# One table of slot numbers placed anew in a single-core layer kernel: jobs and statistics of the first stretches and the last stages

## The chip, the cores and the metric

The kernel runs on one core of one Trainium2 chip. The metric is the device time of one execution in microseconds (us). Three runs of the kernel before took 1712.45, 1713.23 and 1714.37 us; their median is 1713.23 us. The profiled execution is the one of 1712.45 us.

The core has a matrix engine (PE, with its weight loads shown as PEld), a vector engine (DVE), a scalar engine (ACT), a third elementwise engine (POOL) and a queue that issues DMAs (SP). Each engine takes its own instructions in the order in which they are written, and waits on semaphores for the others.

## The reference

Input is x of 4 batches x 2048 positions x 256 features, in float32. What is computed:

```
x = x + 0.5 * ffn(layernorm(x))
x = x + attn(layernorm(x))
x = x + 0.5 * ffn(layernorm(x))

ffn(z)  = z @ W.T + b + (z @ V_r) @ C.T            # 256 -> 256, rank 32
attn(z): q, k, v = split(z @ W_attn)               # 16 heads of 16
  s = (q @ k.T) / 4, causal
  p = (s*s + 1)/1000 for s > 0;  (1 - s/100)/1000 for -100 <= s <= 0
  return (p @ v) @ W_proj
```

There is no division by a row sum, so the attention of a tile can be added up in any order.

## The kernel before, in words

**Chunks and stages.** The 8192 positions are cut into 16 chunks of 512 (four to a batch). Each chunk goes through three stages. Stage A loads x, computes the first layer norm and feed-forward part, then the second layer norm. Stage B projects to q, k and v, splits q and k into three bf16 parts (`split`), and computes per 128 positions a "state", the sum of k times v, from which the linear part of the score function is later formed. Stage C takes the attention's output, projects it, adds x, and computes the third layer norm and second feed-forward part.

**Attention.** It is cut into 64 visits (a batch, a group of 4 heads, a chunk of queries), and a visit into tiles of 128 keys by up to 512 queries; there are 640 tiles, and each is done in two **halves** of 2 heads. For a half, PE writes scores into one of two score buffers (`score<-qs,ks`), then DVE or ACT raises them into `rp` (L1222 on DVE, L1093 on ACT); the next half but one can't be scored until that is done. Tiles on the diagonal need a second operation per head (`lin`, L1228 or L1099) and masks on POOL (L960). Then the raised tile is squared on ACT (L1109, L1113) and, for shared tiles, half of it on POOL (L985), and three tiles later PE multiplies it by v (`y_ps<-rp,vt`). In this text H with a number is a half: tile T consists of H = 2T and 2T + 1.

**Jobs.** Everything else that PE does is a job: z1T, z2T, z3T (transposes of a normalised chunk, L1317), ffn, qT, k, v, kT, state, proj, out. A job is written in pieces into one of two PSUM banks (`bank`), and emptied from it by ACT or DVE. A job can't start before the job two places ahead of it has been emptied. Emptying a `state` (L1208 on DVE) waits for the addition of the state two before it on POOL (L1011, L1013). The statistics of a layer norm are a row of small steps, one slot each, from the slot named `ln1`, `ln2` or `ln3` on: four on DVE (L1247), at +4 the aggregation (L1164), at +6 a square root on ACT (L1122), at +8 a reciprocal on DVE (L1168; for ln2 also the shift, L1171), at +9 to +12 four steps on POOL: for ln2 the normalisation `z` (L945), for ln1 and ln3 the adding of the bias to x (L955).

**The order of the work.** It is written out by hand in slots. `order()` lays a line of slots; in each slot an engine first empties the banks that are due, then does its part of the half in that slot, then its other work, and on PE half, values, then pieces of jobs. A slot has no time: it only says what stands behind what on an engine, and an empty slot costs nothing. The tables give, for each stage, at which slot after the stage's start a job or a layer norm starts. `A_FIRST`, `A_SECOND`, `B_FIRST`, `A_EARLY` and `B_EARLY` serve the first chunks, `A_FULL`, `B_FULL` and `C_FULL` the steady part, which repeats every 80 slots (one half in each), and `C_HALF`, `C_LATE` and `C_SHORT` the last stages, whose starts are in `LATE`. `HALVES_AFTER` says over which slots the first 32 halves are spread; after them every slot holds a half:

```
    first = at + HALVES_AFTER[0]
    second = at + HALVES_AFTER[1]
    halves = 2 * QUADS * NB
    o.put_halves([first + (second - first) * i // halves for i in range(halves)])
```

All later stages are laid relative to `second`.

Of the kernel before, what the change touches and what calls it, by code (L numbers as in the profile page):

```python
# [169 lines left out]

A_FULL = {"z1T": (30, 31), "ffn": (37, 39), "z2T": (64, 64), "ln1": 21, "ln2": 48}
B_FULL = {"qT": (0, 5), "k": (7, 10), "v": (15, 19), "kT": (35, 43), "state": (51, 61, 63, 66)}
C_FULL = {"proj": (22, 26), "ln3": 58, "z3T": (67, 67), "out": (71, 75)}
A_FIRST = {"z1T": (2, 3), "ffn": (6, 10), "z2T": (26, 27), "ln1": 0, "ln2": 15}
A_SECOND = {"z1T": (15, 16), "ffn": (28, 32), "z2T": (49, 50), "ln1": 10, "ln2": 37}
A_EARLY = {"z1T": (12, 13), "ffn": (16, 20), "z2T": (38, 39), "ln1": 5, "ln2": 24}
B_FIRST = {"qT": (0, 12), "k": (2, 6), "kT": (10, 14), "v": (17, 20), "state": (24, 25, 26, 27)}
B_EARLY = {"qT": (4, 6), "k": (7, 8), "kT": (14, 15), "v": (26, 28), "state": (34, 35, 36, 37)}  # L180
C_HALF = {"proj": (0, 7), "ln3": 11, "z3T": (12, 12), "out": (22, 26)}
C_LATE = {"proj": (0, 4), "ln3": 13, "z3T": (9, 10), "out": (18, 24)}
C_SHORT = {"proj": (0, 4), "ln3": 9, "z3T": (9, 10), "out": (18, 22)}


LENGTHS = (36, 51, 42)
HALVES_AFTER = (36, 33)


PLACES = (9, 47, 14, 80)  # L190
ENDS = 3
LATE = (1053, 1086, 1146, 1196, 1231)

AGGR, SCALES, ROOT, NORM, BIAS = NB, NB + 4, NB + 2, NB + 5, NB + 5

# [77 lines left out]
def order():  # L273
    o = Order()
    o.stage(0, o.stretch(LENGTHS[0]), A_FIRST)
    at = o.stretch(LENGTHS[1])
    o.stage(0, at, B_FIRST)
    o.stage(1, at, A_SECOND)
    first = at + HALVES_AFTER[0]
    third, fourth, steady, period = PLACES  # L280
    at = o.n
    o.stage(1, at, B_EARLY)
    o.stage(2, at, A_EARLY)

    second = at + HALVES_AFTER[1]
    halves = 2 * QUADS * NB
# [3 lines left out]
    for c, at in ((2, third), (3, fourth)):  # L290
        o.stage(c, second + at, B_EARLY)
        o.stage(c + 1, second + at, A_EARLY)
    for c in range(CPB, NCH):
        step = c - CPB + 1
        o.stage(c, second + steady + period * step, B_FULL)
        if c + 1 < NCH:
            o.stage(c + 1, second + steady + period * step, A_FULL)
        if step >= ENDS:
            o.stage(step - ENDS, second + steady + period * step, C_FULL)
    done = NCH - CPB + 1 - ENDS  # L300
    for c in range(done, NCH - 1):
        o.stage(c, second + LATE[c - done], C_HALF if c < NCH - 2 else C_LATE)
    assert o.next_half == 2 * len(WORK)
    o.drain = o.n
    o.stretch(LAG + 9)
    o.stage(NCH - 1, o.stretch(32), C_SHORT)
    o.again = o.n
    for c in range(NCH, 2 * NCH):
        o.stage(c, o.stretch(40), C_SHORT)
    o.finish()  # L310
# [1182 lines left out]
```

## Time and profile before

| what | value |
|---|---|
| median of three runs | 1713.23 us |
| profiled execution, its own time | 1712.45 us |
| its span in the trace | 1710.7 us |
| PE busy | 1592.4 us (93%) |
| ACT busy | 1368.1 us (80%) |
| DVE busy | 1327.1 us (78%) |
| POOL busy | 1247.7 us (73%) |
| chain that ended last, by engine | PE 69%, DVE 17%, ACT 7%, issue 4%, POOL 3% |
| mean granted PE clock | 0.988 of full |

The span is the time from the first to the last instruction in the trace; 1.75 us of the execution lie outside it. A share of the span is an average over stretches with different limits, so it has to be read stretch by stretch. A gap of PE in the timeline names what released it. The granted clock (PEclk) is 1.00 at 2.4 GHz and 0.50 at 1.2 GHz.

### The profile page before, as it was taken

The page shows a single profiled execution, that of the slowest core. Times are in us where ns is not written, and L with a number is a line of the kernel's source. Part 1 is how long each engine was busy: PE and PEld are TensorE (multiplying, and loading weights), DVE is VectorE, ACT ScalarE, POOL GpSimd, SP SyncE. Part 2 cuts the span into 40 slices and gives each one's busy share as a digit, 9 for nine tenths or more (in the row PEclk, how much of TensorE's full clock was granted, in tenths as well). Part 3 has the DMA queues.
Part 4 walks back from the last instruction along what each step waited for, and adds up shares of the span by engine and source line. Part 5 has one row for each costly group of instructions (what it writes and reads, how often), then busy time and mean ns, then how long its engine had stood idle before and what let it go on. Part 6 is the DMA issues. An engine that isn't in the chain of part 4 may idle for free.

```text
span 1710.7 us, 67555 instructions
## 1 busy us (share of the span) xinstructions
PE 1592.4 (93%) x27158; PEld 813.7 (48%) x27158; DVE 1327.1 (78%) x3276; ACT 1368.1 (80%) x2182; POOL 1247.7 (73%) x1319
## 2 busy tenths in 40 slices
PE   5698999999998999999998999999999899999997
PEld 3353444444455545545455554544445554444443
DVE  4577777878788787887878678787878768788885
ACT  2366778899887888888887888898888789788883
POOL 1577687877778787776868787687777878667663
PEclk8899999999999999999999999999999999999999
DMA  2654643423346453333435544334333545323311
GB/s 88 180 165 117 179 133 96 128 86 120 89 114 180 140 154 113 114 107 94 131 107 168 162 118 132 116 100 131 124 109 106 162 137 155 105 81 85 91 46 55
DMA packets 183381, 206.16 MB, mean 121 GB/s; under 512 B 27164, under 2 KB 157076, under 8 KB 181276
## 3 DMA queue, kind: packets, MB, share of 16 engines
q1 hardware_dynamic: 183068, 201.77, 39.9%
q8 instruction: 222, 3.64, 0.9%
q14 instruction: 91, 0.75, 0.1%
HBM read 123.26 MB, written 76.30 MB: 117 GB/s over the span
## 4 chain that ended last, share of the span: by engine, by line
PE 69%; DVE 17%; ACT 7%; issue 4%; POOL 3%; DMA 0%; SPq 0%; ACTq 0%; POOLq 0%; DVEq 0%
PE y_ps L1289 26%; PE score L1289 21%; PE bank L1289 18%; DVE rp L1222 11%; PE bank L1317 3%; DVE lin L1228 3%; ACT rp L1093 2%; ACT rp L1113 2%; DVE bnst_ln L1247 1%; POOL rp L985 1%; ACT rp L1109 1%; PE bank L1359 1%; DVE x L1186 1%; ACT parts L1073 0%; POOL z L945 0%
## 5 line engine op out<-in xcount | busy, mean ns | idle before, releaser
L1222 DVE TENSOR_SCALAR rp<-score 128x512 f32<-128x512 f32 (+3 forms) x1728 | 965.0, 585 | 266.2 <-PE score L1289 262.2
L985 POOL TENSOR_TENSOR rp<-rp 128x1024 f32<-128x1024 f32 (+3 forms) x416 | 723.5, 1747 | 97.6 <-DVE rp L1222 86.2
L1289 PE MATMUL score<-qs,ks 96*32 96x512 bf16 (+3 forms) x10240 | 722.6, 349 | 53.4 <-DVE lin L1228 29.9
L1289 PE MATMUL y_ps<-rp,vt 128*16 128x512 f32 (+3 forms) x5120 | 594.4, 532 | 13.5 <-ACT rp L1113 5.1
L1093 ACT ACTIVATE rp<-score 128x512 f32<-128x512 f32 (+3 forms) x832 | 439.8, 570 | 203.6 <-PE score L1289 200.2
L1289 PEld LDWEIGHTS score<-qs,ks 96*32 96x32 bf16 x10240 | 295.4, 96 | 430.8 <-DVE rp L1222 191.6
L1109 ACT ACTIVATE rp<-rp,rise 128x1024 f32<-128x1024 f32 (+3 forms) x416 | 444.2, 1096 | 4.7 <-POOL rp L960 4.7
L960 POOL TENSOR_SCALAR_AFFINE_SELECT rp<-rp 128x256 f32<-128x256 f32 (+1 forms) x384 | 184.6, 481 | 239.8 <-ACT rp L1093 149.1
L1113 ACT ACTIVATE rp<-rp 128x2048 f32<-128x2048 f32 (+2 forms) x224 | 328.9, 1468 | 3.4 <-POOL rp L960 3.3
L1228 DVE SCALAR_TENSOR_TENSOR lin<-score,slope_mask 128x128 f32<-128x128 f32 x768 | 214.0, 279 | 0.0
L1289 PEld LDWEIGHTS y_ps<-rp,vt 128*16 128x16 f32 x5120 | 137.6, 96 | 105.3 <-issue 19.9
L1289 PE MATMUL bank<-w_qkv,z2T 128*32 128x256 f32 x2048 | 151.5, 379 | 0.8 <-ACT parts L1073 0.8
L1289 PE MATMUL y_ps<-lin,vt 128*16 128x128 f32 x2048 | 106.3, 274 | 0.0
L1289 PEld LDWEIGHTS y_ps<-lin,vt 128*16 128x16 f32 x2048 | 62.4, 96 | 80.0 <-issue 67.5
L1289 PEld LDWEIGHTS bank<-w_qkv,z2T 128*32 128x32 f32 x2048 | 68.0, 109 | 68.0 <-issue 43.8
L568 POOL TENSOR_TENSOR parts<-rest,parts 128x512 bf16<-128x512 f32 x56 | 65.5, 1170 | 44.2 <-ACT parts L570 43.2
L1289 PE MATMUL bank<-w_out,y_c 128*32 128x256 f32 x1024 | 77.9, 379 | 1.6 <-DMA y_c<-y_sb 1.6
L1289 PE MATMUL bank<-w_ffn,zT 128*32 128x256 f32 x1024 | 74.6, 393 | 3.6 <-DVE st_add L1208 2.1
L1289 PE MATMUL bank<-w_ffn,z3T 128*32 128x256 f32 x1024 | 76.9, 379 | 0.8 <-ACT z3T L1048 0.8
L566 POOL TENSOR_TENSOR rest<-qkT,parts 128x512 f32<-128x512 f32 x56 | 65.7, 1173 | 15.5 <-ACT parts L1073 15.3
L1099 ACT ACTIVATE lin<-score 128x128 f32<-128x128 f32 x256 | 75.5, 295 | 0.0
L1289 PE MATMUL y_ps<-qT,st 66*16 66x128 f32 x2048 | 68.9, 272 | 1.8 <-issue 1.8
(93 smaller groups left out, 1258.1 us busy)
## 6 DMA issues: line engine op xcount, KB each, us to landing
ks<-part_scratch SPq DMA_DIRECT2D x648, 64.0 KB, 2.4
qs<-part_scratch SPq DMA_DIRECT2D x384, 64.0 KB, 2.4
part_scratch<-parts SPq DMA_DIRECT2D x14, 1536.0 KB, 6.0
vt<-v_scratch SPq DMA_DIRECT2D x102, 128.0 KB, 2.7
state_scratch<-st_new SPq DMA_DIRECT2D x16, 528.0 KB
x_sb<-in_L_attn_x_dram SPq DMA_DIRECT2D x16, 512.0 KB, 4.3
x_scratch<-x SPq DMA_DIRECT2D x16, 512.0 KB, 5.3
qT_scratch<-qkT SPq DMA_DIRECT2D x16, 512.0 KB, 3.3
```

The lines of the kernel that those rows point to most:

```text
L566: ins = eng.tensor_tensor(rest[side][:], qkT[:, i, :], parts[:, i, 0, :], ALU.subtract)
L568: ins = eng.tensor_tensor(parts[:, i, 2, :], rest[side][:], parts[:, i, 1, :], ALU.subtract)
L960: pool.affine_select(out=block, in_=block, compare_op=ALU.is_ge, fill=fill, base=0, pattern=[[0, heads_in_it], [1, P]], channel_multiplier ...
L985: pool.tensor_tensor(half, half, half, ALU.mult).then_inc(squared["pool"], 1)
L1093: nc.scalar.activation(rp[T % RP_BUFS][:, 2 + v, off:CH], score[H % S_BUFS][:, v, off:CH], ACT.Relu).then_inc(raised["act"], 1)
L1099: nc.scalar.activation(lin[D % L_BUFS][:, 2 + v, :], score[H % S_BUFS][:, v, off:off + P], ACT.Copy, scale=SLOPE, bias=ONE).then_inc(lin_d ...
L1109: nc.scalar.activation(part, part, ACT.Square, bias=rise[:]).then_inc(squared["act"], 1)
L1113: nc.scalar.activation(whole, whole, ACT.Square).then_inc(squared["act"], 1)
L1222: nc.vector.tensor_scalar(rp[T % RP_BUFS][:, 2 * u + v, off:CH], score[H % S_BUFS][:, v, off:CH], 0.0, RISE, ALU.max, ALU.add).then_inc(ra ...
L1228: nc.vector.scalar_tensor_tensor(lin[D % L_BUFS][:, 2 * u + v, :], score[H % S_BUFS][:, v, off:off + P], ONE / SLOPE, slope_mask[:, 0, :], ...
L1289: return nc.tensor.matmul(*args, start=start, stop=stop, skip_group_check=True)
L1317: ins = nc.tensor.transpose(dst[:, P * blk:P * blk + P], src[:, blk, P * i:P * i + P], ident[:])
```

## The change

Numbers in the tables are changed, and nothing else: no instruction is added or taken out on any engine, and no line of code but these is touched.

```
-A_FULL = {"z1T": (30, 31), "ffn": (37, 39), "z2T": (64, 64), "ln1": 21, "ln2": 48}
+A_FULL = {"z1T": (31, 31), "ffn": (37, 39), "z2T": (64, 64), "ln1": 21, "ln2": 48}
-C_FULL = {"proj": (22, 26), "ln3": 58, "z3T": (67, 67), "out": (71, 75)}
+C_FULL = {"proj": (22, 26), "ln3": 60, "z3T": (67, 67), "out": (71, 75)}
...
-HALVES_AFTER = (36, 33)
+HALVES_AFTER = (37, 41)
...
-LATE = (1053, 1086, 1146, 1196, 1231)
+LATE = (1053, 1084, 1148, 1197, 1231)
```

`HALVES_AFTER` spreads the first 32 halves over 55 slots (73 to 127) where it was 48 (72 to 119), while the jobs of chunks 1 and 2 in that stretch keep their slots. So fewer halves stand ahead of each of these jobs: z2T of chunk 1 starts behind H7 where it was H9, its qT behind H11 (H13), its first state behind H28 (H33), and z2T of chunk 2 behind H31, both parts in one slot (H37 and H38). In A_FIRST, ln2 moves by 1 slot and z2T by 2, with no other work between; in A_SECOND, ln1 moves from 10 to 14.

In the early stages from then on, A_EARLY has z1T at (13, 14) for (12, 13) and z2T at (39, 39) for (38, 39), and B_EARLY v at (24, 28) for (26, 28) and the states at (34, 35, 37, 37) for (34, 35, 36, 37). In the last stages, C_HALF has out at (24, 28) for (22, 26), C_LATE z3T at (10, 10) for (9, 10) and out at (20, 26) for (18, 24), C_SHORT z3T at (10, 10) for (9, 10) and out at (15, 23) for (18, 22).

**POOL at the second layer norm of chunk 1.** `L945` is the normalisation of one quarter of the chunk, `L960` and `L985` are masks and the squaring of tiles. In the order before, from the squaring of tile 2 on:

```order
L985 TENSOR_TENSOR rp<-rp 128x2x256
L960 AFFINE_SELECT rp<-rp 128x4x128
L945 TENSOR_SCALAR z<-x,rstd_ln,shift 128x256 x3
L960 AFFINE_SELECT rp<-rp 128x2x128
L960 AFFINE_SELECT lin<-lin 128x256
L960 AFFINE_SELECT rp<-rp 128x2x128
L985 TENSOR_TENSOR rp<-rp 128x1024
L945 TENSOR_SCALAR z<-x,rstd_ln,shift 128x256
```

and in the order of the change, from the same instruction on:

```order
L985 TENSOR_TENSOR rp<-rp 128x2x256
L945 TENSOR_SCALAR z<-x,rstd_ln,shift 128x256 x3
L960 AFFINE_SELECT rp<-rp 128x4x128
L945 TENSOR_SCALAR z<-x,rstd_ln,shift 128x256
L960 AFFINE_SELECT rp<-rp 128x2x128
L960 AFFINE_SELECT lin<-lin 128x256
L960 AFFINE_SELECT rp<-rp 128x2x128
L985 TENSOR_TENSOR rp<-rp 128x1024
```

Three normalisations now stand ahead of the mask of tile 3 (H7), and the fourth ahead of the masks and the squaring of tile 4 (H9).

**PE from the last state of chunk 1 to z2T of chunk 2.** `bank<-v_sb,k_sb` is a state, `bank<-ident,z` is z2T. Before:

```order
L1289 MATMUL bank<-v_sb,k_sb 2x64
L1289 MATMUL score<-qs,ks 32x512 x8
L1317 MATMUL bank<-ident,z 128x128 x4
L1289 MATMUL score<-qs,ks 32x384 x8
L1289 MATMUL y_ps<-rp,vt 16x512 x4
L1317 MATMUL bank<-ident,z 128x128 x4
L1289 MATMUL score<-qs,ks 32x384 x8
```

With the change:

```order
L1289 MATMUL bank<-v_sb,k_sb 2x64
L1289 MATMUL score<-qs,ks 32x128 x8
L1317 MATMUL bank<-ident,z 128x128 x8
L1289 MATMUL score<-qs,ks 32x512 x8
L1289 MATMUL y_ps<-rp,vt 16x384 x4
L1289 MATMUL y_ps<-lin,vt 16x128 x4
L1289 MATMUL score<-qs,ks 32x512 x16
```

The states and z2T now stand in front of H32, among the small halves of the last first-chunk visit, where they stood among the wide halves behind it.

**DVE at the third layer norm of the steady part** (here chunk 0). `BN_STATS bnst_ln<-x_0` is its statistics, `BN_AGGR` its aggregation, `st_add` the emptying of a state. Before, from the fourth of its statistics on:

```order
L1247 BN_STATS bnst_ln<-x_0 128x6
L1208 TENSOR_TENSOR st_add<-bank,smask 66x256
L1222 TENSOR_SCALAR rp<-score 128x256
L1228 SCALAR_TENSOR_TENSOR lin<-score,slope_mask 128x128
L1222 TENSOR_SCALAR rp<-score 128x256
L1228 SCALAR_TENSOR_TENSOR lin<-score,slope_mask 128x128
L1164 BN_AGGR mv_ln<-bnst_ln 128x2 x4
```

With the change, from the second of its statistics on:

```order
L1247 BN_STATS bnst_ln<-x_0 128x6
L1208 TENSOR_TENSOR st_add<-bank,smask 66x256
L1222 TENSOR_SCALAR rp<-score 128x256
L1228 SCALAR_TENSOR_TENSOR lin<-score,slope_mask 128x128
L1222 TENSOR_SCALAR rp<-score 128x256
L1228 SCALAR_TENSOR_TENSOR lin<-score,slope_mask 128x128
L1247 BN_STATS bnst_ln<-x_0 128x6 x2
```

Two statistics and the aggregation stand one tile later, behind the 256 wide halves.

## Rows read from the trace of the kernel before

**Rows 1.** Windows of the span: busy time of each engine, granted clock, DMA.

```profile
core 0: us, PE busy (x) PEld busy (x) DVE busy (x) ACT busy (x) POOL busy (x), PEclk, DMA share, GB/s
60.00:84.00 24.00, 14.27 (x180) 7.15 (x176) 14.08 (x46) 10.01 (x20) 11.64 (x18) 0.72 0.76 228
84.00:125.50 41.50, 39.67 (x864) 24.33 (x852) 34.56 (x105) 27.91 (x58) 29.70 (x43) 1.00 0.53 159
...
134.00:320.00 186.00, 172.66 (x2907) 86.34 (x2904) 143.63 (x329) 149.94 (x252) 139.40 (x152) 0.99 0.43 123
320.00:1450.00 1130.00, 1085.70 (x18920) 559.95 (x18916) 904.19 (x2250) 963.08 (x1547) 878.43 (x927) 1.00 0.43 126
```

**Rows 2.** Timeline of POOL, 69 to 81 us: start, length, operation, count, [idle before].

```profile
70.09 1.04 POOL L985 TENSOR_TENSOR rp<-rp 128x512 f32<-128x512 f32 x1
73.42 0.64 POOL L960 TENSOR_SCALAR_AFFINE_SELECT rp<-rp 128x512 f32<-128x512 f32 x1 [2.29 <-DVE rp L1222]
74.05 1.62 POOL L945 TENSOR_SCALAR z<-x,rstd_ln,shift 128x256 f32<-128x256 f32 x3
...
77.48 1.89 POOL L985 TENSOR_TENSOR rp<-rp 128x1024 f32<-128x1024 f32 x1
79.36 0.56 POOL L945 TENSOR_SCALAR z<-x,rstd_ln,shift 128x256 f32<-128x256 f32 x1
```

**Rows 3.** Timeline of PE, 72 to 84 us.

```profile
72.27 1.32 PE L1289 MATMUL score<-qs,ks 96*32 96x128 bf16 x16
...
80.06 1.94 PE L1317 MATMUL bank<-ident,z 128*128 128x128 f32 x8 [5.02 <-POOL z L945]
```

**Rows 4.** Timeline of DVE, 70 to 71 us: the shift of that layer norm.

```profile
70.71 0.45 DVE L1171 SCALAR_TENSOR_TENSOR shift<-mv_ln,rstd_ln 128x4 f32<-128x4 f32 x1
```

**Rows 5.** Windows of the stretch behind the first wait.

```profile
80.00:84.00 4.00, 3.94 (x36) 2.65 (x40) 1.42 (x4) 2.23 (x3) 0.00 (x0) 0.50 0.55 154
```

**Rows 6.** Timelines of PE, POOL and DVE, 125 to 130 us.

```profile
127.92 0.50 PE L1289 MATMUL bank<-v_sb,k_sb 128*2 128x64 f32 x16 [2.36 <-issue]
...
129.47 1.11 PE L1317 MATMUL bank<-ident,z 128*128 128x128 f32 x4
...
125.77 1.89 POOL L985 TENSOR_TENSOR rp<-rp 128x1024 f32<-128x1024 f32 x1
...
128.17 2.47 POOL L1013 TENSOR_TENSOR st_new<-st_new,st_add 66x256 f32<-66x256 f32 x3
...
129.00 0.42 DVE L1208 TENSOR_TENSOR st_add<-bank,smask 66x256 f32<-66x256 f32 x1 [5.32 <-POOL st_new L1013]
```

**Rows 7.** Timeline of DVE, 108 us: ffn of chunk 2 emptied.

```profile
108.10 0.88 DVE L1186 SCALAR_TENSOR_TENSOR x<-bank,rstd_ln,x_sb 128x256 f32<-128x256 f32 x2 [1.60 <-issue]
```

**Rows 8.** Timeline of PE at z2T of chunks 3 and 4.

```profile
197.01 0.66 PE L1317 MATMUL bank<-ident,z 128*128 128x128 f32 x4 [1.82 <-DVE st_add L1208]
...
253.75 0.66 PE L1317 MATMUL bank<-ident,z 128*128 128x128 f32 x4 [1.47 <-DVE st_add L1208]
```

**Rows 9.** Timeline of DVE: the middle step of a split, twice.

```profile
103.17 0.43 DVE L572 CAST parts<-rest 128x512 bf16<-128x512 f32 x1
...
164.46 2.00 DVE L572 CAST parts<-rest 128x512 bf16<-128x512 f32 x1
```

**Rows 10.** Third layer norm of chunk 1: window, then timelines of DVE and PE.

```profile
527.60:535.20 7.60, 6.23 (x163) 4.08 (x160) 7.60 (x29) 5.32 (x11) 6.90 (x13) 1.00 0.84 271
...
528.45 0.74 DVE L1247 BATCH_NORM_STATS2 bnst_ln<-x 128x6 f32<-128x256 f32 x2
...
533.79 0.36 DVE L1164 BATCH_NORM_AGGREGATE mv_ln<-bnst_ln 128x2 f32<-128x6 f32 x4
```

**Rows 11.** Timelines of ACT and PE, 1677 to 1697 us.

```profile
1677.14 0.60 ACT L1048 ACTIVATE z3T<-bank 128x512 f32<-128x512 f32 x1 [0.69 <-PE bank L1317]
...
1686.12 0.61 PE L1289 MATMUL bank<-w_ffn,z3T 128*32 128x256 f32 x8
...
1692.66 3.66 PE L1289 MATMUL bank<-w_out,y_c 128*32 128x256 f32 x64 [1.58 <-DMA y_c<-y_sb]
```

More of the change, by code:

```diff
@@ L169 @@
 COUNT = {"z1T": 2, "z2T": 2, "z3T": 2, "qT": 2, "k": 2, "kT": 2, "state": NB, "v": 2, "ffn": 2, "out": 2, "proj": 2}
-A_FULL = {"z1T": (30, 31), "ffn": (37, 39), "z2T": (64, 64), "ln1": 21, "ln2": 48}
+A_FULL = {"z1T": (31, 31), "ffn": (37, 39), "z2T": (64, 64), "ln1": 21, "ln2": 48}
 B_FULL = {"qT": (0, 5), "k": (7, 10), "v": (15, 19), "kT": (35, 43), "state": (51, 61, 63, 66)}
-C_FULL = {"proj": (22, 26), "ln3": 58, "z3T": (67, 67), "out": (71, 75)}
-A_FIRST = {"z1T": (2, 3), "ffn": (6, 10), "z2T": (26, 27), "ln1": 0, "ln2": 15}
-A_SECOND = {"z1T": (15, 16), "ffn": (28, 32), "z2T": (49, 50), "ln1": 10, "ln2": 37}
-A_EARLY = {"z1T": (12, 13), "ffn": (16, 20), "z2T": (38, 39), "ln1": 5, "ln2": 24}
+C_FULL = {"proj": (22, 26), "ln3": 60, "z3T": (67, 67), "out": (71, 75)}
+A_FIRST = {"z1T": (2, 3), "ffn": (6, 10), "z2T": (24, 27), "ln1": 0, "ln2": 16}
+A_SECOND = {"z1T": (15, 16), "ffn": (28, 32), "z2T": (49, 50), "ln1": 14, "ln2": 37}
+A_EARLY = {"z1T": (13, 14), "ffn": (16, 20), "z2T": (39, 39), "ln1": 5, "ln2": 24}
 B_FIRST = {"qT": (0, 12), "k": (2, 6), "kT": (10, 14), "v": (17, 20), "state": (24, 25, 26, 27)}
[L180 to L183, printed above, removed]
+B_EARLY = {"qT": (4, 6), "k": (7, 8), "kT": (14, 15), "v": (24, 28), "state": (34, 35, 37, 37)}
+C_HALF = {"proj": (0, 7), "ln3": 11, "z3T": (12, 12), "out": (24, 28)}
+C_LATE = {"proj": (0, 4), "ln3": 13, "z3T": (10, 10), "out": (20, 26)}
+C_SHORT = {"proj": (0, 4), "ln3": 9, "z3T": (10, 10), "out": (15, 23)}
 LENGTHS = (36, 51, 42)
-HALVES_AFTER = (36, 33)
+HALVES_AFTER = (37, 41)
 PLACES = (9, 47, 14, 80)
 ENDS = 3
-LATE = (1053, 1086, 1146, 1196, 1231)
+LATE = (1053, 1084, 1148, 1197, 1231)
 AGGR, SCALES, ROOT, NORM, BIAS = NB, NB + 4, NB + 2, NB + 5, NB + 5
```

## The prediction

> **What bounds the kernel now.** I read the windows of the span first [rows 1]. From 134 us on PE is busy for 93% to 96% of each window, at the full granted clock; the reader sees that all matmuls have to pass, and that only a few us in a hundred are open to a better order. The same holds from 84 to 125.5 us (39.67 of 41.5 us busy). The window from 60 to 84 us is different: PE is busy for 14.27 of 24 us, at a mean clock of 0.72. Then I read PE's timeline for its gaps, and for each of them the timeline of the engine that ended it. Three kinds matter.
>
> First, PE stands still for 5.02 us until 80.06 [rows 3]: z2T of chunk 1 waits for the fourth normalisation on POOL, which stands behind the squaring of 77.48 [rows 2]. The window behind it shows PE at a granted clock of 0.50 for 4 us, so 3.94 us of work pass there that take half of that, 1.97 us, at 1.00 [rows 5]. Second, at z2T of chunk 2 DVE stands for 5.32 us in front of a state, whose bank it may empty only when POOL has added the state two before; POOL comes to that at 128.17, behind another squaring [rows 6]. PE had stopped for 2.36 us in the last state (by "issue", so the profile names no releaser), and starts z2T at 129.47, just when DVE has finished at 129.42. The same wait costs 1.82 and 1.47 us at z2T of chunks 3 and 4 [rows 8]. Third, in the steady part the gaps are many and small. I looked at one place where DVE has no free time: at the third layer norm of chunk 1 DVE is busy for 7.60 of 7.60 us, and PE for 6.23 [rows 10].
>
> **The change part by part.** No instruction goes or comes, so each term is a wait that shrinks or grows.
>
> (a) z2T of chunk 1. POOL ends the squaring of tile 2 at 71.13 (70.09 + 1.04) and the shift is ready at 71.16 (70.71 + 0.45) [rows 2, 4]. Now POOL lets three normalisations wait for a mask that itself waits 2.29 us for H7. In the new order the three follow at once: 71.16 + 1.62 = 72.78. Then come the mask of H7 (0.64) and the fourth z (0.56): 73.98, against 79.92 now. One delay is to be added: the statistics of this layer norm move ahead of H2, which pushes H3 and with it ACT's part by about two statistics, 0.74 us for two in [rows 10]. So z is ready at about 74.7, and PE starts z2T there and not at 80.06, 5.3 us sooner. What PE now does before its gap (H8, the values of tile 1, H9), between the end of H7 at 73.0 and 75.04 (80.06 - 5.02), 2.0 us, falls behind it [rows 3]. Gain 3.3 us. Ends: nothing, if another wait stands at the same place, and 7.0 us, if the gap and the slow window behind it go altogether (5.02 + 1.97).
>
> (b) States of chunk 1. With the first state five halves earlier, its addition on POOL stands behind one squaring of 1.04 us [the length in rows 2] and not behind those of 1.89 us for H35 and H37 [rows 6]. But PE also has only small halves with which to fill the time until z2T, and z2T is now both parts in one slot. The gap was 2.36 us, and the granted clock fell after it; together between 0 and 4 us. I take 1.5, nearer to the lower end, since by name that gap is no wait for POOL.
>
> (c) ffn of chunk 2. DVE waits 1.60 us to empty it, until the bias has been added on POOL at 108.0 [rows 7]. In the new order three of the four additions come before the next squaring's turn. Between 0 and 1.6; I take 0.8.
>
> (d) z2T of chunks 3 and 4 start one half later, the states 2 and 3 in one slot: one more half covers the same wait. Between 0 and 3.3 (1.82 + 1.47) [rows 8]; I take 1.5.
>
> (e) The cost of (b). Four states and eight transposes leave the halves behind H32 for a stretch where PE is already 96% busy [rows 1]. Sixteen of the 24 matmuls of a state took 0.50 us [rows 6], so I estimate a state at 0.6, and four transposes take 0.66 [rows 8]: 4 x 0.6 + 2 x 0.66 = 3.7 us that lengthen that stretch at most, and the halves from H33 to H44, then without a job, run at the pace of ACT and DVE and give back only part of it. Between 0 and +3.7; I take +1.0.
>
> (f) kT of chunks 2 and 3 now stands between the parts of z1T, so that ffn waits for z1T's emptying; and DVE's splits of chunk 1 run beside POOL's additions. The middle step of a split took 0.43 us with POOL idle and 2.00 us with POOL working [rows 9]. Between 0 and +2.5; PE has ffn to do meanwhile, so I take +0.7.
>
> The Trainium skill bears on (f): "GPSIMD Engine Reference", section 1 and Key points, says that POOL shares its SBUF interfaces with VectorE and disturbs VectorE's instructions that use both ports. By that rule the moved splits of chunk 1 would be slowed and (f) would stand at its upper end, 2.5, and the forecast at 1706.8 where it is 1705.0 by my value. The two rows agree with it on the instruction, but not on who waits for it.
>
> (g) The steady part. ln3 moves by two slots in ten stages. In the stretch where DVE is full, two statistics (0.74) and the aggregation (0.36) leave, 1.1 us [rows 10], for one where DVE has room, since z2T and z3T keep PE busy there. At most ten times 1.1, 11 us, at least -4 (0.4 a stage, if they now stand in front of a half that PE waits for). PE's own gap in that stretch is 1.37 us (7.60 - 6.23), at a diagonal visit, which is the worst; in most stages less of it can go. I take 0.2 a stage, 2.0 us. z1T at 31 for 30 moves one transposition job past one half, where PE has no gaps: 0.
>
> (h) The tail. H1273 stood on ACT behind the emptying of z3T, for which ACT waited 0.69 us; now it goes first. And out of chunk 14 starts behind the last values and not ahead, which takes one piece, at most 0.61 us, out of the way of the last y, on which PE waits for 1.58 us at 1692.66 [rows 11]. Between 0 and 1.6; I take 0.8. The shifts of LATE by 1 or 2 slots and of out by 2: 0, within 1 us to either side. ln1, ln2 and z2T in the first two tables move past nothing that waits: 0.
>
> Sum: 3.3 + 1.5 + 0.8 + 1.5 - 1.0 - 0.7 + 2.0 + 0.8 = 8.2 us less. The profiled execution took 1712.45 us (span 1710.7 and 1.75 outside), so 1704.3 for one like it; the median stands 0.8 above, so I predict 1705.0.
>
> **Rivals.**
> 1. The first wait goes with its clock. If z is ready before PE comes to it and the state's wait is gone, (a) is 7.0 and (b) 4: 6.2 us more, 1698.8. For it speaks that POOL's chain has no wait left; against it, that PE comes there at 73.0 and my sum has z at 74.7. The Trainium skill ("TensorE: Matmul & The Clock Gate", The HAM clock gate) has the clock fall only after the array has been idle for long enough, and by it a gap of 1.7 us would cost no clock. That agrees with the gap of 1.82 us [rows 8], behind which four transposes took 0.66 us, against 1.94 for eight behind the gap of 5.02; by it the 2.0 us of the slow window would be gained on top, 1703.0, where my sum leaves them lost.
> 2. The gain is given back at once. The halves of the first chunk are bound by DVE (14.08 of 24 us) and the jobs only fill PE's time between them. If (a) only moves the wait to H10 and (b), (c) and (g) are nothing, there remain 3.3 + 0.8 (h) + 0.8 (half of d) - 3.7 = 1.2 us, 1712.0. That is no change by the bound of 0.2%, 3.4 us, which is about what a measurement of this kernel tells from none.
> 3. Slower: PE's own work binds. The states and z2T (3.7 us) lie in a stretch that PE already fills, and the halves from H33 on don't run faster for it, since ACT squares and raises for as long as PE scores. With (f) at its end, 2.5, and (g) turned, 4, that is 10.2 against 6.4 of (a), (b), (c) and (h): 3.8 slower, 1717. It decides if (g) costs more than 0.4 us a stage while (e) is whole. For it: DVE is full in that stretch. Against it: the aggregation certainly leaves it.
> 4. The order changes but the waits with it do not, as each is bound to the same semaphores; then 1713.2. Against it the order of POOL, where z is no longer behind a squaring.
>
> **How the numbers follow.** My case 0.57, rival 1 0.15, rival 2 0.12, rival 3 0.09, rival 4 0.07. The own range of my case is 1701 to 1709, from halving or doubling (a) and (g). To leave out 2 in 10 at most, the range reaches towards both sides to 1698.5 and 1712. Faster by over 0.2% (below 1709.8): 0.53 of my case's 0.57, rival 1's 0.15 and 0.02 of rival 2, 0.70. Within 0.2%: the rest, 0.21. Slower: rival 3, 0.09.
>
> **What would show it.** (a) right: the gap of PE before z2T of chunk 1 is 1 to 2.5 us and z2T starts near 75; wrong: it stays over 4. (b) and (e): the window around z2T of chunk 2 has under 1.5 us of gap, and PE shows new gaps behind ACT from H33 to H44. (d): the waits on st_add at z2T of chunks 3 and 4 are under 1 us. (g): PE's busy share from 320 us on rises by 0.2% at the same work, and DVE has free time where it was full; wrong if that stretch is as long as now. (h): the last projection's wait for y stays, and comes 0.5 us sooner against the last half. The forecast as a whole is wrong if the early part, up to the first halves of batch 0's last visits, is less than 3 us shorter.

## The result, and the profile after

| | before | after |
|---|---|---|
| median of the runs on one chip | 1712.52 us (7 runs) | 1700.14 us (7 runs) |
| lowest to highest | 1710.07 to 1714.37 | 1697.35 to 1704.44 |
| profiled execution: time, span | 1712.45, 1710.7 | 1698.37, 1696.6 |

The ratio of after to before is 0.9937, 95% interval 0.9923 to 0.9950, that is 10.8 us less (the medians are 12.4 apart). The forecast was 1705.0, in a range from 1698.5 to 1712.0: the sign and the range hold, the time came out 4.9 us below it (as a gain, 8.2 us forecast and 10.8 measured). The profiled execution of after is 1.8 us below its own median, so its trace shows a little more than the kernel gains.

The windows of after, on three of the stretches of [rows 1] and with its columns:

```profile
60.00:84.00 24.00, 17.14 (x236) 8.11 (x228) 16.04 (x54) 11.20 (x22) 12.22 (x19) 0.72 0.73 220
84.00:125.50 41.50, 35.44 (x688) 20.57 (x680) 30.73 (x92) 23.81 (x48) 28.16 (x40) 0.92 0.59 184
...
320.00:1450.00 1130.00, 1085.81 (x19056) 562.01 (x19050) 905.71 (x2253) 965.17 (x1551) 884.08 (x930) 1.00 0.43 127
```

The first window gained 2.87 us of PE's work and the second lost 4.23. The last is the odd one: PE is busy just as long as before (1085.81 against 1085.70 us), with 136 more matmuls in the window. So there the gain is not idle time that went. The same work takes less of PE (in part because of a fall of the clock that this execution of before had and that of after had not, last section).

Where the time goes is best read half for half. H48 is the 49th half of the run, and its end is the end of its second raise on DVE or ACT. The table is worked out from the timelines of those engines: the end of each half against the kernel before, in us. Minus is earlier.

| kernel | H0 | H16 | H20 | H48 | H96 | H130 | H970 | H1050 | H1170 | H1279 |
|---|---|---|---|---|---|---|---|---|---|---|
| after | -1.4 | -3.8 | +4.1 | 0.0 | -4.3 | -5.9 | -10.1 | -11.4 | -10.9 | -13.9 |
| e_early | -1.1 | -3.5 | +4.4 | +0.4 | -3.6 | -5.2 | -5.8 | -5.1 | -5.1 | -5.0 |
| e_steady | +0.7 | +0.8 | +0.8 | +0.9 | +0.8 | +2.0 | -0.5 | -1.8 | -1.4 | -1.4 |
| e_late | -0.4 | -0.6 | -0.6 | -0.5 | -0.6 | +0.6 | +1.8 | +0.9 | +1.1 | -1.8 |

Not everything in it belongs to the change. In kernels that don't differ there, H0 ends between 1.5 us earlier and 0.7 us later than in before. The jumps between H970 and H1050, and that of e_steady and e_late at H130, come from a clock that falls in some executions and not in others (last section).

**The first wait.** The timelines of POOL and PE in after, answering to [rows 2, 3], and the granted clock around them:

```profile
70.50 1.64 POOL L945 TENSOR_SCALAR z<-x,rstd_ln,shift 128x256 f32<-128x256 f32 x3
72.09 0.64 POOL L960 TENSOR_SCALAR_AFFINE_SELECT rp<-rp 128x512 f32<-128x512 f32 x1
72.72 0.56 POOL L945 TENSOR_SCALAR z<-x,rstd_ln,shift 128x256 f32<-128x256 f32 x1
...
73.42 1.08 PE L1317 MATMUL bank<-ident,z 128*128 128x128 f32 x4 [2.20 <-POOL z L945]
```

```profile
66.00:71.00 5.00, 3.73 (x40) 1.51 (x40) 3.44 (x14) 3.25 (x7) 3.30 (x6) 0.50 0.89 324
...
72.00:78.00 6.00, 4.58 (x32) 2.19 (x32) 1.72 (x5) 0.60 (x1) 1.27 (x3) 0.50 0.94 266
78.00:80.00 2.00, 2.00 (x38) 0.90 (x36) 0.67 (x2) 1.73 (x5) 0.00 (x0) 0.81 0.78 218
```

The three z follow the shift at once, the mask and the fourth z come behind them, and PE waits 2.20 us where it waited 5.02. But the clock stands at 0.50 until about 78.6 us all the same. This wait did not bring it down: the first of these windows shows it at 0.50 from 66 us on, 5 us ahead of the wait, among the small gaps of the first halves. In before it had fallen there too (0.50 from 67 to 73 us), had come back (1.00 from 74 to 77), and fell a second time inside the gap of 5.02 us.

**The wait that is new.** DVE, POOL and PE around 100 us, where DVE's split of kT of chunk 1 now stands:

```profile
97.72 2.26 DVE L566 TENSOR_TENSOR rest<-qkT,parts 128x512 f32<-128x512 f32 x1
100.01 0.84 DVE L572 CAST parts<-rest 128x512 bf16<-128x512 f32 x1
100.89 1.09 DVE L568 TENSOR_TENSOR parts<-rest,parts 128x512 bf16<-128x512 f32 x1
...
97.54 1.90 POOL L985 TENSOR_TENSOR rp<-rp 128x1024 f32<-128x1024 f32 x1
99.39 3.18 POOL L955 TENSOR_TENSOR x_sb<-x_sb,bias_half 128x256 f32<-128x256 f32 x3
...
103.39 0.41 PE L1289 MATMUL score<-qs,ks 96*32 96x256 bf16 x4 [2.45 <-DVE lin L1228]
```

```profile
103.00:110.00 7.00, 6.03 (x68) 2.62 (x72) 4.21 (x16) 3.20 (x6) 5.17 (x8) 0.54 0.67 192
```

All three steps run beside POOL and take 4.19 us (2.26 + 0.84 + 1.09), and the raises of H19 and H20 stand behind them (H18 ends at 97.0, H19 at 103.7). The scores of H21 need the buffer of H19: PE waits 2.45 us for it and then works at a clock of 0.54 for 7 us.

**States of chunk 1**, answering to [rows 6]:

```profile
121.72 1.10 POOL L945 TENSOR_SCALAR z<-x,rstd_ln,shift 128x256 f32<-128x256 f32 x2
122.78 1.59 POOL L1013 TENSOR_TENSOR st_new<-st_new,st_add 66x256 f32<-66x256 f32 x2
...
123.61 0.42 DVE L1208 TENSOR_TENSOR st_add<-bank,smask 66x256 f32<-66x256 f32 x1 [2.78 <-POOL st_new L1013]
...
124.09 0.66 PE L1317 MATMUL bank<-ident,z 128*128 128x128 f32 x4 [1.90 <-DVE st_add L1208]
```

DVE stands for 2.78 us and not 5.32, but still for POOL, where the state now waits behind the last two z.

**kT between the parts of z1T, and z2T of chunks 3 and 4.** Before, the half behind kT of chunk 2 waited 2.81 us for DVE, and the clock fell behind it. The place in before (two rows that stand in no group so far), then the same place in after, with z2T of chunks 3 and 4 [rows 8]:

```profile
168.27 0.93 PE L1289 MATMUL score<-qs,ks 96*32 96x512 bf16 x8 [2.81 <-DVE lin L1228]
...
168.20:172.20 4.00, 3.80 (x40) 1.99 (x44) 2.66 (x7) 0.61 (x1) 3.86 (x6) 0.64 0.06 28
```

```profile
161.97 0.66 PE L1359 MATMUL bank<-ident,k_sb 128*128 128x128 f32 x4 [1.48 <-ACT parts L1073]
...
167.58 0.93 PE L1289 MATMUL score<-qs,ks 96*32 96x512 bf16 x8 [1.80 <-DVE lin L1228]
...
194.32 0.66 PE L1317 MATMUL bank<-ident,z 128*128 128x128 f32 x4 [0.60 <-DVE st_add L1208]
...
249.13 0.66 PE L1317 MATMUL bank<-ident,z 128*128 128x128 f32 x4 [0.40 <-DVE st_add L1208]
...
167.50:171.50 4.00, 3.79 (x66) 1.99 (x70) 3.86 (x9) 0.59 (x1) 3.86 (x6) 1.00 0.05 22
```

The reader sees the order turned: kT's part now waits 1.48 us, and the long wait shrinks by 1.01. In the 4 us behind it PE does 66 matmuls and not 40, since the clock stays at 1.00.

**The tail**, answering to [rows 11]:

```profile
1678.46 3.66 PE L1289 MATMUL bank<-w_out,y_c 128*32 128x256 f32 x64 [1.27 <-DMA y_c<-y_sb]
```

It starts 8.23 us behind the end of H1279, against 8.59 before: 0.36 us, of which 0.24 reach the end of the span.

### The profile page after: what moved, and what is told of

The parts are those of the page before. It is cut to its first block, busy times and chain, and to the rows that moved or that the text cites. A ratio compares the mean times of both kernels' runs of the same rounds, so it can differ in the third digit from the quotient of the medians.

```text
span 1696.6 us, 67555 instructions
## 1 busy us (share of the span) xinstructions
PE 1583.0 (93%) x27158; PEld 812.6 (48%) x27158; DVE 1329.0 (78%) x3276; ACT 1368.3 (81%) x2182; POOL 1250.2 (74%) x1319
## 4 chain that ended last, share of the span: by engine, by line
PE 69%; DVE 16%; ACT 7%; POOL 4%; issue 4%; DMA 0%; SPq 0%; ACTq 0%; POOLq 0%; DVEq 0%
PE y_ps L1289 26%; PE score L1289 21%; PE bank L1289 18%; DVE rp L1222 10%; PE bank L1317 3%; ACT rp L1093 2%; DVE lin L1228 2%; ACT rp L1113 2%; POOL rp L985 1%; DVE bnst_ln L1247 1%; ACT rp L1109 1%; POOL z L945 1%; PE bank L1359 1%; POOL x_sb L955 1%; ACT parts L1073 1%
## 5 line engine op out<-in xcount | busy, mean ns | idle before, releaser
L985 POOL TENSOR_TENSOR rp<-rp 128x1024 f32<-128x1024 f32 (+3 forms) x416 | 724.2, 1749 | 95.2 <-DVE rp L1222 83.8
L960 POOL TENSOR_SCALAR_AFFINE_SELECT rp<-rp 128x256 f32<-128x256 f32 (+1 forms) x384 | 186.3, 485 | 230.8 <-ACT rp L1093 148.9
```

Of the source, the lines that this page charges most:

```text
L960: pool.affine_select(out=block, in_=block, compare_op=ALU.is_ge, fill=fill, base=0, pattern=[[0, heads_in_it], [1, P]], channel_multiplier ...
L985: pool.tensor_tensor(half, half, half, ALU.mult).then_inc(squared["pool"], 1)
```

## The experiments

"Kernel before" means that only the named numbers are those of after. Ratios are to the kernel before, with their 95% interval; x_ kernels start from after.

**e_early: the first stretches alone.**

```
+HALVES_AFTER = (37, 41)
+A_FIRST, A_SECOND, A_EARLY, B_EARLY as in after; the other tables and LATE as before
```

> Only the tables of the first stretches (HALVES_AFTER, A_FIRST, A_SECOND, A_EARLY, B_EARLY) as in the change; steady and last stages as before. Theory (the parts add up, and the early one is the largest): about 6 us less than before, all of it gained by H128, whose half ended 5.9 us sooner in the changed kernel, and nothing gained behind it. Rival (the drift of 0.4 us a stage behind H130 comes from a shifted phase of the early part and not from ln3): 10 us or more less than before, with the drift there.

Measured 1705.43 us, 0.9963 (0.9950 to 0.9976), 6.3 us less. In the table it follows after up to H130 and is flat from there.

**e_spread: HALVES_AFTER alone**, and **e_early_tables: the four tables without it.**

```
 e_spread:        HALVES_AFTER = (37, 41), all tables as before
 e_early_tables:  HALVES_AFTER = (36, 33), A_FIRST, A_SECOND, A_EARLY, B_EARLY as in after
```

> Only HALVES_AFTER (37, 41), every table as before. Theory (the distance of the jobs of chunks 1 and 2 from the halves is what counts): z2T of chunk 1 starts near 74 us and the wait before it is about 2.2 us where it was 5.0; H48 ends as early as in the kernel with all early tables, and the whole takes 2 to 4 us less than before. Rival (the jobs' places within the stages do it): under 1.5 us.

> Only A_FIRST, A_SECOND, A_EARLY and B_EARLY as in the change, HALVES_AFTER as before. The spreading alone made no difference and both together 6 us less. Theory (the spreading wins 2 us before H16 and loses them at H20, and the tables win theirs behind H48: later z2T, earlier v, kT between the parts of z1T): until H48 as before, then 3.5 to 5 us less by H128, and as much in all. Rival (they only work together): under 1.5 us less than before.

Measured 1.0006 (0.9996 to 1.0017) and 0.9983 (0.9974 to 0.9992). Alone the spreading gains nothing that can be measured: its H20 is 4.7 us late and its H48 1.0. The tables alone gain 2.9 us; their H48 is 2.4 us late, and from H48 to H130 they need 120.5 us where before needs 126.0 (after 120.1, e_spread 125.8). So what the tables gain, they gain behind H48, at kT/z1T and z2T of chunks 3 and 4. Together the two give 6.3, more than their sum (1.9). The traces agree in sign with less of it: counted from H0, at H130 e_early is 4.2 us ahead, the tables alone 3.4 ahead and the spreading alone 0.9 behind. What makes the two help each other was not run apart.

**e_steady: A_FULL and C_FULL alone**, **e_z1T: of these only z1T**, **e_ln3: only ln3.**

```
-A_FULL = {"z1T": (30, 31), ...     (e_steady, e_z1T)
+A_FULL = {"z1T": (31, 31), ...
-C_FULL = {..., "ln3": 58, ...      (e_steady, e_ln3)
+C_FULL = {..., "ln3": 60, ...
```

> Only A_FULL and C_FULL as in the change (z1T one slot later, ln3 two slots later). Theory: 0.3 to 0.45 us less in each of the ten stages with an ln3, 3 to 4.5 us in all, and up to H300 no difference. Rival: no more than 1 us, the drift comes from elsewhere.

> Only A_FULL as in the change: z1T of the steady stages one slot later. Theory (PE has no gap there, and all of the steady gain is ln3's): every eightieth half as in the kernel before within 0.1 us a stage. Rival: a part of the 3.7 us that the steady tables won between H130 and H1050 appears here.

> The kernel before with only C_FULL's ln3 at 60 instead of 58, as in the changed kernel; z1T stays at (30, 31). Theory A (formed on e_steady and e_z1T): the steady gain comes from z1T alone, whose two jobs now stand in one slot: eight 128x128 transposes in a row on TensorE cost 1.02 us where two groups of four with a score group between them cost 0.59 + 0.58 us and the score group 0.55 instead of 0.43, so about 0.27 us a stage goes, eleven times. Then ln3 alone gives nothing: ratio 1.000 (within 0.0007), and half for half the trace stays level with the kernel before. Rival B (my prediction on record: ln3 gives 0.2 us in each of ten stages, z1T nothing): ratio about 0.9988, -2.0 us. Rival C (both needed): 1.000 here as well, and then e_z1T would have had no drift, which it had (from -1.05 to -4.1 us between halves 130 and 650).

Measured: e_steady 0.9985 (0.9974 to 0.9996), 2.6 us less; e_z1T 1710.58 us in its one run, so that only its trace can be used; e_ln3 1.0008 (0.9996 to 1.0020). In one stage (H311 to H326, at 490 us) e_z1T gets ahead by 0.3 us, and PE has no gap there in either kernel. PE's timeline in before:

```profile
493.29 0.39 PE L1289 MATMUL y_ps<-lin,vt 128*16 128x128 f32 x8
493.61 0.66 PE L1317 MATMUL bank<-ident,x_sb 128*128 128x128 f32 x4
494.20 0.62 PE L1289 MATMUL score<-qs,ks 96*32 96x512 bf16 x8
494.75 0.66 PE L1317 MATMUL bank<-ident,x_sb 128*128 128x128 f32 x4
495.33 0.29 PE L1289 MATMUL score<-qs,ks 96*32 96x128 bf16 x8
495.46 1.03 PE L1289 MATMUL y_ps<-rp,vt 128*16 128x512 f32 x8
```

and in e_z1T:

```profile
491.62 0.39 PE L1289 MATMUL y_ps<-lin,vt 128*16 128x128 f32 x8
491.84 0.60 PE L1289 MATMUL score<-qs,ks 96*32 96x512 bf16 x8
492.38 1.10 PE L1317 MATMUL bank<-ident,x_sb 128*128 128x128 f32 x8
493.40 0.29 PE L1289 MATMUL score<-qs,ks 96*32 96x128 bf16 x8
493.52 1.03 PE L1289 MATMUL y_ps<-rp,vt 128*16 128x512 f32 x8
```

From the same value matmul to the same y it is 2.17 us (495.46 - 493.29) and 1.90 (493.52 - 491.62). The work is the same; the eight transpositions stand in one group (1.02 us to the next start) and not in two (0.59 and 0.58), and one change from other work to transpositions is gone. By starts, 0.15 us of it lie in the transpositions (1.17 against 1.02) and 0.10 in the value matmuls ahead of them (0.32 against 0.22); the group of 512 wide scores takes the same (0.55 and 0.54), and not 0.43 as the expectation of e_ln3 had it.

One stage could be chance, so here are all eleven: the time from the end of H151 to the end of H166, around z1T, and so on every 80 halves. The median of the five kernels with z1T at (31, 31) and kT as in before (after, e_steady, e_z1T, x_split, x_early2) lies below that of the seven with (30, 31), e_ln3 among them: by 0.25 to 0.36 us in ten stages (in the first, 18.21 to 18.22 against 18.47 to 18.48), by 0.08 in one, 2.9 us in all. That fits e_steady's 2.6. The gain is z1T's; e_ln3's interval excludes the 2.0 us that the prediction gave to ln3.

**e_late: C_HALF, C_LATE, C_SHORT and LATE alone**, and **e_out: only the out jobs of C_HALF and C_LATE.**

```
-C_HALF = {..., "out": (22, 26)}   C_LATE = {..., "out": (18, 24)}
+C_HALF = {..., "out": (24, 28)}   C_LATE = {..., "out": (20, 26)}      (e_out)
```

> Only C_HALF, C_LATE, C_SHORT and LATE as in the change. Theory: equal to before until H1060, then 2 to 3 us less, since in the changed kernel H1260 against H1050 ended 2.7 us sooner than before. Rival (my forecast): 0.8 us, all of it in the last 40 us of the span.

> The kernel before with only the out jobs of C_HALF and C_LATE two slots later (24, 28 and 20, 26), LATE and everything else as before. Theory A: the gain of the late part (e_late: 0.9981, -2.9 us) comes from the emptying of out on VectorE (0.87 us each), which stood before raises that TensorE waited for; with the out jobs alone about -1.5 to -2 us of it is there (ratio 0.9988 to 0.9991), and the gaps of TensorE near 1655 and 1660 us (0.39 and 0.40 us) shrink. Rival B (LATE's shifts of one or two slots carry it): ratio 1.000, the gaps stand. Rival C (my prediction on record): out shifts are worth nothing within 1 us: 0.9994 to 1.0006.

Measured: e_late 0.9981 (0.9969 to 0.9993), 3.3 us less, all of it between H1170 and H1279; e_out 0.9992 (0.9980 to 1.0003), by its trace 1.25 us ahead in the same stretch. The interval of e_out holds no change too, so this rests on the trace. DVE and PE in before:

```profile
1652.83 0.87 DVE L1202 SCALAR_TENSOR_TENSOR x<-bank,rstd_ln,x 128x256 f32<-128x256 f32 x2
...
1658.60 0.87 DVE L1202 SCALAR_TENSOR_TENSOR x<-bank,rstd_ln,x 128x256 f32<-128x256 f32 x2
...
1655.43 0.40 PE L1289 MATMUL score<-qs,ks 96*32 96x512 bf16 x4 [0.39 <-DVE lin L1228]
...
1660.12 0.40 PE L1289 MATMUL score<-qs,ks 96*32 96x512 bf16 x4 [0.40 <-DVE rp L1222]
1660.71 0.40 PE L1289 MATMUL score<-qs,ks 96*32 96x512 bf16 x4 [0.20 <-DVE rp L1222]
```

and DVE in e_out, where PE has none of these three gaps:

```profile
1651.29 0.88 DVE L1202 SCALAR_TENSOR_TENSOR x<-bank,rstd_ln,x 128x256 f32<-128x256 f32 x2 [0.39 <-PE bank L1289]
...
1656.49 0.88 DVE L1202 SCALAR_TENSOR_TENSOR x<-bank,rstd_ln,x 128x256 f32<-128x256 f32 x2 [0.73 <-PE bank L1289]
```

Emptying out's bank had stood between raises that PE waited for (0.99 us in the three gaps). Two slots later DVE has to wait for the job itself. Another 0.27 us comes from z3T of the last chunks, in one slot now: from the y at 1675.47 to the y at 1678.62 it is 3.15 us in before, and from 1661.89 to 1664.77, 2.88, in after, with no gap of PE in either. All six kernels with z3T joined need 18.82 or 18.83 us from H1262 to H1279, the other eight 19.08 to 19.10. The rest of e_late lies elsewhere: from H1170 to H1250 it gains 1.5 us (87.85 against 89.39), where e_out gains nothing (89.52). It belongs to the shifts of LATE, or to these and out together; they weren't run apart.

**x_split: the split of chunk 1's kT later.** After, but DVE's part of it stands six slots behind the job and not one, so that the raises of H19 and H20 go first. The DMAs that need it move by four or five slots.

```
-s = x.empty_at + (1 if x.chunk < EARLY else SPLIT[step])
+s = x.empty_at + (6 if (x.kind, x.chunk, x.i) == ("kT", 1, 0) else 1 if x.chunk < EARLY else SPLIT[step])
...
-s = x.empty_at + ((12, 2)[x.chunk] if x.chunk < DIRECT else ...
+s = x.empty_at + ((12, 6)[x.chunk] if x.chunk < DIRECT else ...
...
-put(x.empty_at + 2, "first k", x.chunk)
+put(x.empty_at + (7 if x.chunk else 2), "first k", x.chunk)
```

> The changed kernel, with DVE's split of chunk 1's first kT five slots later (behind the halves H18 to H20 and POOL's squaring and bias additions) and the DMAs that need it four or five slots later. Theory (the wait of 2.45 us before H20 in the changed kernel is DVE's split, slowed by POOL's work beside it from 1.8 to 4.3 us, and the granted clock falls behind that wait): the wait before H20 goes, the steps take 0.68, 0.43 and 0.69 us again, H32 is raised 3 to 5 us sooner than in the changed kernel and the whole takes 3 to 5 us less than it, about 16 less than before. Rival (the wait only moves: the ffn of chunk 2 or the loads for H32 are late next): under 1 us less than the changed kernel.

Measured 1700.43 us, 0.9935 (0.9921 to 0.9949): 11.1 us less than before, where the theory asked for 16 (0.9906, outside the interval). Against after no change is seen, and one of 3 us would not be. DVE and PE:

```profile
103.66 1.62 DVE L566 TENSOR_TENSOR rest<-qkT,parts 128x512 f32<-128x512 f32 x1
...
103.36 0.24 PE L1289 MATMUL score<-qs,ks 96*32 96x128 bf16 x4 [1.55 <-DVE lin L1228]
...
103.00:110.00 7.00, 6.19 (x104) 3.08 (x108) 6.90 (x20) 2.52 (x3) 5.89 (x8) 1.00 0.33 98
167.00:171.00 4.00, 3.81 (x40) 1.92 (x44) 2.55 (x6) 0.61 (x1) 3.86 (x6) 0.60 0.07 31
```

The wait of 2.45 us is gone, the clock stays at 1.00, and H20 ends 2.0 us sooner than in after (103.5 against 105.5). But in front of H22 there is a wait of 1.55, and at H48 only 0.5 us is left: a wait that goes is replaced by the next. At H64 it is 1.1 us behind after, and that is another matter: PE waits 1.80 us at 167.06 as after does at 167.58, but here the clock is at 0.60 behind it (the last row) and in after at 1.00, so that H56 to H64 take 15.3 us and not 13.7. Nor does the steps' length come back, as expected: beside POOL the subtraction takes 1.62 us and not 0.68.

**x_early2: the long splits for chunks 2 and 3.** After, with the splits of these chunks placed as in the steady part.

```
-EARLY = CPB
+EARLY = 2
```

> The changed kernel, with chunks 2 and 3 split as the steady chunks are (first and third step on POOL, the second on ACT, spread over slots) and no step on DVE. Theory (DVE's splits of chunks 2 and 3, with a middle step of 2.00 us beside POOL, make the gaps of 0.64, 1.80 and 1.48 us between 150 and 168 us, and a slow stretch of the clock): H64 and H104 come 3 to 5 us sooner than in the changed kernel. Rival (POOL has no room for four splits of 3 steps a chunk there, and its squares come late): the gaps move to y_ps behind POOL, and it is equal or slower by up to 3 us.

Measured 1700.60 us, 0.9933 (0.9919 to 0.9946): no change either. Counted from H0 it is 2.0 us ahead of after at H64 and 1.6 at H130 (265.85 - 64.57 against 265.47 - 62.58), but 1.6 behind at H1279 (1673.8 - 64.6 against 1670.2 - 62.6). Of these 3.2 us, 2.5 are lost at the two stops of the last section (1.2 from H610 to H690, 1.3 from H930 to H1010), where this execution has a clock of 0.57 for 4 us behind each and that of after 1.00. So the edit may be worth the 1.6 us of H130; these measurements can't tell that from nothing.

**x_kT: kT of the steady stages joined as well**, and **x_merge: that, and z1T and kT of the first chunks.**

```
-B_FULL = {..., "kT": (35, 43), ...
+B_FULL = {..., "kT": (43, 43), ...                                          (both)
+A_SECOND "z1T": (16, 16)   A_EARLY "z1T": (14, 14)   B_EARLY "kT": (15, 15)   (x_merge)
```

> The changed kernel with one more number: B_FULL's kT at (43, 43) instead of (35, 43), so that the two jobs of kT of each of the twelve steady stages stand in one slot, as z1T's now do. Theory A (each separate group of 128x128 transposes between other work costs TensorE about 0.27 us more than when it is joined to another, whichever job it is): -0.27 x 12 = -3.2 us against the changed kernel, a ratio to the kernel before of 0.9918 instead of 0.9937. Rival B (z1T's gain has to do with its slot and the emptying around it, not with the joining): no change, 0.993 to 0.994. Rival C (with both jobs in one slot the two banks are freed late, and VectorE's split of kT0 then stands beside that of kT1): TensorE gets a wait of 0.3 us or more behind slot 43, and the time is at or above the changed kernel's, 0.9937 to 0.996.

> x_kT and, in the first stretches too, both jobs of z1T (chunks 1 to 4: 16, 16 and 14, 14) and of kT (chunks 1 to 3: 15, 15) in one slot. Theory A (joining pays on TensorE wherever it is the bound): up to 7 more x 0.27 = -1.9 us where TensorE is the bound there, so 0.9907 to 0.9918. Rival B (in the first stretches scalar and vector engine are waited for; two banks to be emptied at once before the next job lengthen z1T to ffn): the same as x_kT or up to 3 us more, 0.992 to 0.994.

Measured: x_kT 1717.56 us, 1.0041 (1.0028 to 1.0054), 17.4 us slower than after; x_merge 1718.24 us, 1.0040 (1.0026 to 1.0053). My rule of the joined groups did not carry over. Of the theories the third comes nearest: its wait behind slot 43 is there, but the time lies far above its range (to 0.996), and what makes the wait is not the split. DVE and PE in x_kT, and the answering row of after below them:

```profile
505.99 0.66 PE L1359 MATMUL bank<-ident,k_sb 128*128 128x128 f32 x4 [0.42 <-DVE x L1186]
...
509.71 1.27 DVE L1234 TENSOR_REDUCE qk_max<-qkT 128x1 f32<-128x512 f32 x2
...
511.66 0.24 PE L1289 MATMUL score<-qs,ks 96*32 96x128 bf16 x4 [1.08 <-DVE lin L1228]
```

```profile
507.92 0.24 PE L1289 MATMUL score<-qs,ks 96*32 96x128 bf16 x4 [0.48 <-DVE lin L1228]
```

The two parts don't join at all: between them PE waits 0.42 us for the bank, which DVE empties of ffn in that same slot. And the two reductions of kT (1.27 us) now stand together in front of one half, so that PE waits 1.08 us where it waited 0.48. That is 1.0 us (0.42 + 0.60) at this stage. From H130 to H1050 x_kT loses 17.1 us against after, 1.4 a stage on average; the other stages were not read. In the first stretches x_merge gains 2.5 us on x_kT from H16 to H48 and gives 2.8 back by H130.

## Why the prediction came out so

The total was right in sign and within its range, but that it came near is luck, because errors of both signs met: one of 4.4 us too good up to H48, against gains behind it that were put at a cost or at nothing. Step by step:

- **(a)** "z is ready at about 74.7, and PE starts z2T there": 73.28 and 73.42; 1.35 us of that is the earlier H0, so the place is right to within 0.1. Gain by H16: 2.5 us counted from H0 (3.8 - 1.35), forecast 3.3. PE's gap is 2.20 us and not 1.7, and the second part of z2T stands behind H8, which the sum did not see. The missing 0.8 fits the clock: H8 and the values behind z2T ran at 0.50 (73.4 to 77.1 us in after), where before runs them at 0.62 to 1.00 (73 to 75 us). That the slow clock would not be gained was right, but not for the reason given: the slow stretch of after begins before this wait.
- **(b), (c), (e) and the split in (f)** were to give 0.6 us together (1.5 + 0.8 - 1.0 - 0.7). From H16 to H48 they cost 3.8 (52.6 us for these halves against 48.8; kernels that don't differ from before there need 48.8 to 49.8). This is the largest error. A part of it is where (f) said "PE has ffn to do meanwhile, so I take +0.7": PE ran out of other work at 100.94 and had 2.45 us of wait and then a clock of 0.54. The sign "under 1.5 us of gap" at z2T of chunk 2 failed as well: 2.11 (1.90 and 0.21). And no new gaps behind ACT appeared from H33 to H44. The Trainium skill ("GPSIMD Engine Reference", section 1 and Key points) would have put (f) at its upper end; the subtraction, 2.26 us beside POOL at 97.72 and 0.68 in before with POOL idle, agrees with it. Yet x_split, which takes that wait away, still needs 51.9 us from H16 to H48: 0.7 of the 3.8 hang on it. The larger part comes with the spreading: e_spread alone, with no table changed, needs 51.7. There (e), put at +1.0 of at most 3.7, is the term that can hold it, but which of (b), (c) and (e) it is was not run apart. The wait on POOL's bias of (c) is gone; DVE waits for PE in its place (2.76 us at 109.48).
- **kT between the parts of z1T**, the other half of (f), was booked as a cost. At its place is the largest gain of the first stretches: from H56 to H72 after gains 2.5 us (-0.25 to -2.71). These halves take 26.6 to 26.8 us in all seven kernels with the old tables and 24.3 to 24.6 in after, e_early, e_early_tables and x_kT (x_early2 and x_merge change the place itself). The wait of 2.81 us is 1.01 shorter, and the clock behind it, which fell in all seven (0.58 to 0.64 over 4 us), stays at 1.00 in these four; in x_split it falls all the same, and the halves take 25.7. So the shorter wait gives about 1.0 us each time, and the clock the rest most times. The edit was run only together with its tables, of which v moves here too. I had read the row of DVE there [rows 9] and not the gap of PE that it leads to.
- **(d)** 1.5 forecast; the waits fell from 1.82 to 0.81 (0.60 and 0.21) and from 1.47 to 0.62 (0.40 and 0.22), as the sign asked, and after gains 1.1 and 1.3 us at the two places: 2.4, inside the bounds.
- **(g)** 2.0 forecast, 2.6 measured (e_steady), for the wrong reason. The step that failed is "z1T at 31 for 30 moves one transposition job past one half, where PE has no gaps: 0": a PE that is never idle still gets faster when two groups of transpositions become one. ln3, on which the 2.0 stood, gives nothing. The aggregation did leave the full stretch (DVE is busy for 6.90 of 7.60 us from 513.0 to 520.6 us in after), but no time came of it. The sign "PE's busy share from 320 us on rises by 0.2%" failed: it is the same, and the work in it is more.
- **(h)** The tail gave 0.24 us behind H1279 and 0.27 ahead of it, 0.5 of 0.8, and the second by z3T in one slot, not by H1273's place on ACT, for PE had no gap there. "The shifts of LATE by 1 or 2 slots and of out by 2: 0, within 1 us" is the under-sized term: 3.3 us measured (e_late).
- **The rivals.** Rival 1 (1698.8) came near in time, but not by its mechanism, since the slow stretch of the clock stayed and the wait on the state is still 1.90 us. Rival 2's thought, that the early gain is given back at once, is what happened up to H48 (+1.3 counted from H0); it was wrong from there on. Rival 3's price for moving the states is likely the loss of e_spread up to H48 (+1.0 against before); its sum leaves out (d), with whose 1.5 us it would be 2.3 slower and not 3.8.

By the ratios, the three parts run alone give 6.3 + 2.6 + 3.3 = 12.2 us where the whole gives 10.8, with an interval of 2.3 to either side: they add up.

## What to carry to other kernels

Where PE is the bound and never idle, look at the order of the kinds of matmul, and not only at gaps: here joining two groups of four transpositions saved 0.27 us of 2.17. But join them only where both banks are free and the work that hangs on them isn't doubled in one slot; x_kT lost 17.4 us with the same edit on another job. In a stretch bound by several engines in turn, the value of a wait that is removed has to be read a few dozen steps later, since of x_split's 2.0 us at H20 0.5 were left at H48. And where a gain or loss of 1 to 3 us appears between two traces, look first whether the clock fell in one of them.

## What the runs showed of the hardware

**One wait, three clocks.** PE stops at its 14704th matmul of 27158 in 13 of the 14 kernels and at its 21458th in all of them, for 1.6 to 3.0 us, with "issue" as reason. Behind the second of them the granted clock differs between executions. Before, after and e_z1T:

```profile
1342.15 0.51 PE L1289 MATMUL y_ps<-qT,st 66*16 66x128 f32 x10 [1.82 <-issue]
...
1342.10:1348.10 6.00, 5.95 (x95) 3.63 (x99) 1.98 (x12) 4.36 (x10) 2.85 (x5) 0.72 0.47 111
```

```profile
1332.34 0.51 PE L1289 MATMUL y_ps<-qT,st 66*16 66x128 f32 x10 [2.48 <-issue]
...
1332.30:1338.30 6.00, 5.96 (x140) 3.79 (x141) 3.69 (x16) 4.73 (x11) 4.08 (x7) 1.00 0.46 113
```

```profile
1338.70:1344.70 6.00, 5.96 (x75) 4.33 (x75) 1.21 (x5) 3.46 (x8) 2.85 (x5) 0.50 0.38 104
```

In the same 6 us PE does 95, 140 or 75 matmuls. The shorter wait (1.82) lost clock and the longer (2.48) did not. Behind the same wait of 1.82 us e_out keeps its clock, and needs 1.6 us less than before from H970 to H1050; e_z1T, at 0.50, needs 2.8 more than e_spread, whose stop is as long (2.37) and whose clock stays. So such a fall costs 1 to 3 us, and 1.3 us of the difference between the two profiled executions (H970 to H1050) come with it and are none between the kernels. The Trainium skill ("TensorE: Matmul & The Clock Gate", The HAM clock gate) has short gaps cost no clock. These traces bear that out in some executions only: z2T's wait of 1.90 us at 124.09 in after costs none, the wait of 1.47 us at z2T of chunk 4 leaves the clock at 1.00 in before and at 0.63 in e_steady, and that of 2.45 us at 103.39 is followed by 0.50.

**A stop at nearly fixed instructions.** Those two places are the same matmul by count and by name in kernels whose waits differ; but x_merge runs through the first of them without a stop, and the order around both is nearly the same in all kernels, so count and place can't be told apart. What makes the stops was not tried. The stop of 2.36 us in [rows 6], also by "issue", did not stay at its count: it is at the 1441st in before, at the 1321st in x_split (1.28 us), and in after none is seen.

**A slow vector instruction beside POOL.** The same subtraction of 128x512 on DVE took 0.68 us in before with POOL idle, and beside POOL at work 1.19 (before, at 163.24), 1.62 (x_split) and 2.26 us (after). POOL is slowed as well: its squaring of 128x1024, 1.89 us in [rows 2], took 2.35 beside the cast of 2.00 us in [rows 9].
